# Aggregation units of 128 instead of 256 places, and the choice of experts for two blocks at a time

## The reference

```
h     = x @ W_gat                               # 4 heads x 4
e     = leaky_relu(a_src[src] + a_dst[dst])     # per edge and head
ee    = exp(e - max over the edges of dst)
agg   = segment_sum(h[src] * ee / segment_sum(ee, dst), dst) + b_gat
score = mean over heads of layernorm(agg)       # one score for each of 4 experts
w     = softmax of the two best scores; the two others get 0
out   = sum over experts of w[e] * (gelu(x @ W1[e] + b1[e]) @ W2[e] + b2[e])
x     = x + out
```

## Time and profile before

| | |
|---|---|
| median of three runs | 4157.47 us (4153.68 to 4172.66) |
| profiled execution | 4160.54 us, its span 4158.8 us |
| first block ends, second starts | about 1320 us |
| third pick of the loop; last additions | 1458.6 us; 4111 us |
| tail: last choice, four steps, stores | 4111 to 4158.8 us |
| busy share of PE, DVE, ACT, POOL | 67%, 78%, 27%, 67% |
| granted PE clock, mean of the span | 0.803 |

### The profile page before, as it was taken

One profiled execution on the slowest core, in us unless ns is written; L12 is line 12 of the kernel. 1 busy time (PEld: TensorE's weight loads), 2 busy tenths in 40 slices (PEclk: granted clock), 3 DMA queues, 4 the chain that ended last, 5 costly groups with the idle time before them and its releaser, 6 DMA issues.

```text
span 4158.8 us, 58181 instructions
## 1 busy us (share of the span) xinstructions
PE 2783.3 (67%) x19194; PEld 2162.5 (52%) x19194; DVE 3235.2 (78%) x5615; ACT 1122.5 (27%) x997; POOL 2780.4 (67%) x2785
## 2 busy tenths in 40 slices
PE   4488433358885277777777777777777776677775
PEld 1255322246563266665655556565565555556553
DVE  8877999988885477777778777787777777777775
ACT  0011000001111233343334333433333333333332
POOL 3000388888875777777777777777777777777771
PEclk8799655568887578888888887888888888888887
DMA  1133211169998921222222222222222222222283
GB/s 54 32 94 94 64 45 45 45 70 122 116 115 119 119 48 41 56 55 51 56 51 56 51 51 51 53 54 41 57 54 51 56 51 51 49 53 45 50 51 17
DMA packets 383237, 253.16 MB, mean 61 GB/s; under 512 B 302146, under 2 KB 337538, under 8 KB 382596
## 3 DMA queue, kind: packets, MB, share of 16 engines
q1 hardware_dynamic: 295284, 220.70, 25.6%
q0 software_dynamic: 87552, 29.20, 9.5%
q10 hardware_dynamic: 144, 0.00, 0.0%
HBM read 179.40 MB, written 70.24 MB: 60 GB/s over the span
## 4 chain that ended last, share of the span: by engine, by line
POOL 31%; issue 15%; DVE 11%; PE 7%; SPq 2%; DVEq 1%; DMA 1%; ACT 0%; ACTq 0%
POOL gath L1219 31%; PE C L1333 2%; DVE acc L1508 2%; PE C L1317 2%; PE A L1356 1%; PE A L1364 1%; SPq L1139 1%; DVE A L1573 1%; DVE nodes L1574 1%; DVE C L1473 1%; DVE picked L1469 1%; PE A L1346 1%; DVEq L1111 1%; DMA tab_d<-nodes 1%; SPq L1186 1%
## 5 line engine op out<-in xcount | busy, mean ns | idle before, releaser
L1219 POOL DMA_INDIRECT gath<-tab_d,src_no x2116 | 1998.3, 944 | 645.9 <-issue 644.0
L1333 PE MATMUL C<-spread,lo_hot 128*128 128x160 f32 x4360 | 844.7, 359 | 711.8 <-DVEq L1510 557.4
L1333 PEld LDWEIGHTS C<-spread,lo_hot 128*128 128x128 f32 x4360 | 769.3, 234 | 845.3 <-DVEq L1510 671.8
L486 POOL DMA_INDIRECT edge_d<-run_slots,slots x544 | 675.7, 1242 | 600.3 <-ACT run_slots L685 437.8
L1317 PEld LDWEIGHTS C<-damp,lo_hot_t 128*128 128x128 f32 x4384 | 547.1, 202 | 115.1 <-issue 115.1
L1317 PE MATMUL C<-damp,lo_hot_t 128*128 x4384 | 555.6, 283 | 53.6 <-ACT lo_hot_t L1238 36.5
L1508 DVE TENSOR_TENSOR acc<-acc,C 128x160 f32 x1090 | 347.8, 319 | 267.3 <-DVE C L1473 100.3
L598 PE MATMUL C<-wide_rec,hot_lo 128*128 128x136 f16 x2048 | 271.8, 304 | 300.3 <-DVE wide_rec L886 300.3
L598 PEld LDWEIGHTS C<-wide_rec,hot_lo 128*128 128x128 f16 x2048 | 241.8, 123 | 351.5 <-DVE wide_rec L886 294.2
L1495 DVE TENSOR_TENSOR spread<-hi_hot,C 128x2560 f32<-128x2560 f32 x137 | 386.4, 2820 | 4.7
L1271 ACT ACTIVATE nodes<-A,b2s 128x512 f32<-128x512 f32 x196 | 134.7, 687 | 862.4 <-PE A L1356 862.4
(11 more groups left out here) (282 smaller groups left out, 3292.1 us busy)
## 6 DMA issues: line engine op xcount, KB each, us to landing
lo_rows<-lo_d SPq DMA_DIRECT2D x137, 512.0 KB
gath<-tab_d,src_no POOLq DMA_INDIRECT x2116
pixels<-in_x SPq DMA_DIRECT2D x32, 392.0 KB, 7.9
src<-in_x SPq DMA_DIRECT2D x32, 392.0 KB, 9.3
nodes<-t_d SPq DMA_DIRECT2D x98, 128.0 KB
nodes<-x_d SPq DMA_DIRECT2D x98, 128.0 KB, 3.0
out<-nodes SPq DMA_DIRECT2D x784, 16.0 KB
edge_d<-run_slots,slots POOLq DMA_INDIRECT x544
```

The source lines that it names most:

```text
L486: pool.indirect_dma_start(edge_d, bass.IndirectOffsetOnAxis(ap=slots[:, k, c:c + 1], axis=0), run_slots[:, k, c * RUN:(c + 1) * RUN, :].re ...
L1219: pool.indirect_dma_start(gath[:, g % BUFS, j, :], None, node_d if g < BUFS else tab_d, bass.IndirectOffsetOnAxis(ap=src_no[:, t:t + 1], a ...
L1333: mm = pe.matmul(C[:, bank, at:at + HI * VALS], lo_hot[:, g % UNROLL, u * U + j, :], spread[:, u * U + j].rearrange("p h v -> p (h v)"), s ...
```

## The change

A unit becomes one tile (`U` 2 to 1), a group 16 units (`UG` 8 to 16), so a group still has 16 tiles. Padding shrinks: 2132 units of 128 places, 134 groups. Each tile's sums are now added to the table by themselves: the matmul of a tile starts and stops its own PSUM region, a pair is two tiles, and a group has 8 pairs where it had 4. A unit has 32 runs instead of 64, so the sorted list lies over 32 partitions and is loaded four times instead of twice.

The choice of experts is made for two blocks at once (23 times), and for the last three blocks singly. Its scratch tiles hold two blocks; some of them move into `na`, which is free by then. The gate has four buffers instead of two. The steps of a pair of blocks are spread from the group after which the second one is full, at group 6 at the earliest; 63 groups have two steps, 61 of these without a choice.

The core of the diff:

```diff
-U = 2
-UNIT_RUN_BITS = 6
+U = 1
+UNIT_RUN_BITS = 5
-UG = 8
+UG = 16
-FULL_AFTER = [-(-((j + 1) * MAX_UNITS // NB) // UG) for j in range(NB)]
+CHOICES = [(j, j + 1) for j in range(0, NB - 3, 2)] + [(j,) for j in range(NB - 3, NB)]
+FULL_AFTER = [-(-((js[-1] + 1) * MAX_UNITS // NB) // UG) for js in CHOICES]
+for c, js in enumerate(CHOICES):
+    steps = len(js) * EXPERTS
+    begins = max(FULL_AFTER[c], ends)
+    ends = max(FULL_AFTER[c + 1], begins + steps // 2) if c + 1 < len(CHOICES) else NG
+    STEP_AT += [begins + n * (ends - begins) // steps for n in range(steps)]
...
-                for k in range(8):
+                for k in range(16):
                     pool.dma_start(edge_d.rearrange("(p n) e -> p (n e)", p=RUN_ROWS)[:, k * n:(k + 1) * n], zeros_h[0:RUN_ROWS, 0:n].bitcast(F16)).then_inc(s["pads_written"], 16)
...
-                def choose(j):
+                def choose(c):
+                    n = len(CHOICES[c]) * HI
+                    for k, j in enumerate(CHOICES[c]):
+                        rows = slice(k * HI, (k + 1) * HI)
+                        here = acc[:, bass.ds(block_at(dve, j), HI), :]
+                        L(dve.tensor_scalar(stat[:, rows], here[:, :, FEAT:VALS], 1e-16, None, ALU.add))
+                        L(dve.reciprocal(stat[:, rows], stat[:, rows]))
+                        L(dve.tensor_tensor(mine[:, rows].rearrange("p q (h d) -> p q h d", h=HEADS), here[:, :, 0:FEAT].rearrange("p q (h d) -> p q h d", h=HEADS),
+                                            stat[:, rows].rearrange("p q (h d) -> p q h d", d=1).broadcast_to([P, HI, HEADS, DIM]), ALU.mult))
+                    L(dve.tensor_tensor(mine, mine, over(vecs[:, 0, :], FEAT), ALU.add))
...
+                    for k, j in enumerate(CHOICES[c]):
+                        if j >= 4:
+                            dve.wait_ge(s["gate_spread"], (j - 3) * EXPERTS)
+                        dve.tensor_tensor(gate[:, j % 4], rank[:, rows], one[:, rows, 1:2].broadcast_to([P, HI, EXPERTS]), ALU.mult).then_inc(s["gate_ready"], 1)
```

More of the change, by code:

```diff
@@ L111 @@
 assert TILES % P and LO_BANKS <= 4
-FULL_AFTER = [-(-((j + 1) * MAX_UNITS // NB) // UG) for j in range(NB)]
-STEP_AT = [FULL_AFTER[j] + e * (FULL_AFTER[j + 1] - FULL_AFTER[j]) // EXPERTS if j + 1 < NB else NG for j in range(NB) for e in range(EXPERTS)]
+CHOICES = [(j, j + 1) for j in range(0, NB - 3, 2)] + [(j,) for j in range(NB - 3, NB)]
+CHOICE_OF = [c for c, js in enumerate(CHOICES) for j in js]
+FULL_AFTER = [-(-((js[-1] + 1) * MAX_UNITS // NB) // UG) for js in CHOICES]
+STEP_AT, ends = [], 0
+for c, js in enumerate(CHOICES):
[3 more added lines that the diff above has]
+    STEP_AT += [begins + n * (ends - begins) // steps for n in range(steps)]
 LAST_STEP = STEP_AT[EXPERTS - 1::EXPERTS]
-assert FULL_AFTER[NB - 1] == NG and max(STEP_AT.count(g) for g in range(NG)) <= 2
+assert NB % 2 and FULL_AFTER[-1] == NG and max(STEP_AT.count(g) for g in range(NG)) <= 2
 class Signal:
@@ L1069, in build @@
             T, hid, plain, X1 = late[:, 0:2], late[:, 2:4], late[:, 4:6], late[:, 6:6 + X_BUFS]
[L1070 to L1080, removed]
+            gate = tb("gate", [P, 4, HI, EXPERTS])
+            na_row = na[:].rearrange("p q f -> p (q f)")
+            mine_2, square_2 = (na_row[:, k * 2 * HI * FEAT:(k + 1) * 2 * HI * FEAT].rearrange("p (q f) -> p q f", f=FEAT) for k in range(2))
+            half_2 = na_row[:, 4 * HI * FEAT:5 * HI * FEAT].rearrange("p (q f) -> p q f", f=FEAT // 2)
+            beats_2 = na_row[:, 5 * HI * FEAT:5 * HI * FEAT + 4 * HI * EXPERTS * EXPERTS].rearrange("p (k q e f) -> p k q e f", k=2, q=2 * HI, e=EXPERTS)
+            stat_2 = tb("stat", [P, 2 * HI, EXPERTS])
+            logit_2 = tb("logit", [P, 2 * HI, EXPERTS])
+            odds_2 = tb("odds", [P, 2 * HI, EXPERTS])
+            one_2 = tb("one", [P, 2 * HI, 2])
+            root_2 = tb("root", [P, 2 * HI, 2])
+            rank_2 = tb("rank", [P, 2 * HI, EXPERTS])
             beta = tb("beta", [P, EXPERTS])
@@ L1121, in gates_due @@
             def gates_due(g):
-                return [j for j in range(NB) if FULL_AFTER[j] == g + 1]
+                return [c for c in range(len(CHOICES)) if FULL_AFTER[c] == g + 1]
             def steps_due(g):
                 return [(j, e) for j in range(NB) for e in range(EXPERTS) if STEP_AT[j * EXPERTS + e] == g]
-            raw = lo_hot[:].rearrange("p b t l -> p (b t l)").bitcast(F16)[:, 0:PLACES * RUN * FIELDS]
-            RAW_WORDS = PLACES * RUN * FIELDS // 2
+            raw = hots[:].bitcast(F16)[:, 0:PLACES * RUN * FIELDS]
             @block.sync
@@ L1533, in choose @@
+                    L(dve.tensor_tensor(square, mine, mine, ALU.mult))
+                    L(dve.tensor_tensor(mine, mine, over(vecs[:, 1, :], FEAT), ALU.mult))
+                    L(dve.tensor_reduce(one[:, :, 1], square, AX.X, ALU.add))
                     L(dve.tensor_scalar(one[:, :, 1], one[:, :, 1], 1.0 / FEAT, 1e-5, ALU.mult, ALU.add))
```

87 lines of the change are left out of this document (40 added, 47 removed).

## The result

The changed kernel takes 4633.99 us (median of four runs, 4627.83 to 4652.4), the kernel before 4161.98 us in the same comparison: 1.1137 times as long, 95% interval 1.111 to 1.1164.

A forecast was written before the change was run, and what follows sets the result against it. POOL's gathers set the pace before, with DVE's loop under 2% slack, and DVE becomes the bound. The terms sum to +495 us: 4655 by the profile, 4650 by the median, range 4560 to 4760, chance 0.72.

The forecast's parts named there:

- Rival (c): In the loop, POOL goes on setting the pace and DVE adds in its gaps: 4112 us, chance 0.03.
- Additions: On DVE's in-order queue, 521 more pairs of additions at 1.035 us each: +539 us.
- rival (b): On DVE, wait and signal between pairs hide, a pair costs 0.64 us: about 4395 us, chance 0.07.
- Block numbers: DVE's load brings 16 numbers instead of 8, +0.33 us in each of 134 groups: +44 us.
- Choices: On DVE, 49 single choices of experts become 23 double at 14.2 us and 3 single: -154 us.
- Groups fewer: In DVE's loop, 134 groups instead of 137, each 8.25 us without step and additions: -25 us.
- Second steps: DVE waits for PE at second expert steps, 61 groups at 3.3 us, plus later release of PE: +73 us.
- PE late for the picks: PE's scatter ends later behind DVE's additions, so DVE waits 0.4 us a group: +52 us.
- Rival (a): PE's lower clock late in half the groups makes DVE wait 2.25 us a group: about 4895 us, chance 0.18.
- Additions waiting for tiles: The second half's additions waiting for PE's two tiles, priced at nothing: room at full clock, not at the lower.
- Ahead of the loop: Before the loop, larger sorted-list load, 8 casts instead of 4 and a wider table: +14 us together.
- The slack: In the loop, DVE no longer waits for gathered rows: -48 us.

The follow-up runs named there:

- The run with own block numbers: Kernel before, every pair of additions done twice, the second time with block numbers from a second load and own address steps: 4718.41 us, ratio 1.1362.
- The runs before it: Kernel before: every addition twice, 4448.86 us; every pair twice with own wait and signal, 4499.9 us; the second time into the next pair's place, 4497.15 us.
- the runs with PE's idle time moved: Kernel after: eight unused matmuls added behind each group's second pair, 4944.22 us; or expert's first half moved on PE behind the second pair, 5071.75 us.

## Why the prediction was right

4650 us was predicted, 4634 measured, by the mechanism of the forecast: DVE's queue became the bound. Term by term, on the two profiled spans (4650.7 - 4158.8 = +492):

- The bound. POOL waits for rows 3.5 us a group (said: 3 and more), DVE for no gather. Rival (c), POOL going on to set the pace, is out: with half the gathers gone the changed kernel moves by 0.5%.
- Additions, +539. Pairs are 1.04 us apart, the additions hold 682 us. The run with own block numbers carries the price: there 1090 additions and a load add 564 us (said in its expectation: 543). The runs before it say why rival (b) fell: with the wait and the signal shared and no new address a pair is 0.70 us, near the 0.64 of that rival; the rest is 0.11 for the wait and the signal and 0.23 for the address steps, which I had put together. The Trainium skill, "VectorE: DVE Perf Modes", section "The DRAIN you can't avoid", says of copies with a semaphore after each that it costs nothing extra. A wait with a signal of its own was 0.11 us a pair here, and the measurement decides.
- Block numbers, +44: mis-sized, +67. A load of 16 takes 1100 ns, not 597 + 8 x 41.
- Choices, -154: the double one was put at 14.2 us and takes 14.19 in the turn read, 13.9 by the means of the turns, -161.
- Groups fewer, -25. Not measured apart.
- Second steps, +73: mis-sized, +19. The waits are 177.0 us instead of 158.1. In 60 turns with two steps and no choice the second step waits 2.55 us on average, in the 48 before it was 2.56. My 3.3 had put all of the 158 us on those 48, but 19 of them belong to first steps and 17 to the tail; and the 0.5 us for a PE let go later did not come.
- PE late for the picks, +52: mis-sized, +13 (waits of picks without the longest, 47.8 - 31.8 = 16.0 us; before, 39.3 - 36.6 = 2.7). The reason given, low clock in the first half of a turn and full clock at the picks, is what the trace shows: in 128 turns the fourth pair's tiles run at 1.2 GHz 120 times, the eighth's, just ahead of the picks, at 2.4 GHz 124 times. Rival (a) did not come, but the runs with PE's idle time moved are this rival in the flesh, at 4944 and 5072 us against the 4895 I gave it. The Trainium skill's "TensorE: Matmul & The Clock Gate", section "A second HAM failure mode: psum-queue depth-cycling", on which it leaned, agrees with those two runs (granted clock 0.78 and 0.67 in the stretch of the earlier trace rows, where the kernel after has 0.83); in the kernel after only the first half of a turn shows it.
- Additions waiting for tiles: left out of the sum, +53. The 251 waits hold 128.4 us, but 0.25 of each is in the pair's 1.035 already (65.6 remain; before 21.7 and 38 times, 12.2). I had looked for it in the second half; it is in the first. The condition I gave, room at the full clock and none at the lower, held there.
- Ahead of the loop, +14: +33 between the third picks (1458.6 and 1491.8), but most of that is this one execution's. The load's wait grew by 10.2 us (said 11.4). The casts take 8.31 us in fours, 2.05 each, not 1.31 as I had carried over: +11.4 instead of +5.3. The wait for the node rows gave 12.3 back. Together +9. Some 22 us more come from the ranking stage far ahead, whose code is the same (one of its operations starts for the first time at 161.1 and for the last at 435.0 us before, at 163.8 and 459.0 after), and in the other runs of the changed loop the third pick stands at 1459 to 1477 us.
- The slack, -48. As said.

With these sizes: 539 + 67 - 161 - 25 + 19 + 13 + 53 + 33 - 48 = +490 of +492; without the 22 us of this one execution 468, where the medians differ by 472. The terms for the additions, the groups and the slack are the predicted ones in this sum; the terms inside the loop give 457 together, and from the third pick to the last additions it grew by 461 (2652.8 to 3113.8 us). The hit owes something to luck: block numbers, tiles and the start came out 95 us dearer, second steps, picks and choices 100 us cheaper. What was not luck is the additions' term, larger than all the others, read from one turn of DVE.

No run that does all the work beats the kernel before. Double choices with units of 256 equal it, and half of the gathers gone, which leaves work out, gave only 1.15%.

## What to carry to other kernels

Where one engine sets the pace and the next has 2% of slack, price a change on the next one, and by the distance of two starts in a turn, not by busy time: here the addresses, waits and signals between operations were a third of an addition's price (0.34 of 1.035 us a pair). When such an operation is doubled to price it, see that the program does not share its address. And an engine off the path can still cost 438 us by the place of its idle time: look at what it does after each of its long waits in a turn, and who waits for that.

## What the runs showed of the hardware

- A load of numbers into registers took 309 ns for one (the place of a block), and for block numbers 331 for 4, 597 for 8 and 1100 for 16: some 65 ns for each number beyond the fourth.
- An addition at an address from a register: a pair of them started 1.04 us after the pair before it with two new addresses, a wait and a signal; doubling a pair at the same addresses added 0.81 us, and 0.70 where the wait and the signal were shared too.
- A cast of strided 16-bit fields took 2.05 us on 32 partitions, and 1.31 on 64 with 2.2% more elements each. The two also read at another spacing: before, two neighbouring places out of each run of 4, now one out of each. Whether the spacing or the partitions make it dearer, no run separates.
- The pick halves lasted 1.97 us (granted clock 1.00) behind idle times of 1.11 and 1.61 us ahead of the seventh pair, and 3.46 (0.50) behind 2.19 and 2.38. More matmuls in a turn lowered the mean clock (0.83 to 0.78 in the stretch of the earlier trace rows), with the idle time standing elsewhere.
